# Two groups of output lines side by side in the PSUM banks: reordering the matmuls of an image convolution

## The reference

```
res = conv3x3(x, W_id, b_id)
cA, cH, cV, cD = _swt2_level3(x[0])
...
dmt = jnp.concatenate([low_att, high_att], axis=1)
out = jax.nn.leaky_relu(conv3x3(dmt, W_enc, b_enc), 0.01)
return out + res
...
x = x + _L0_conv_ref(_gn(x), ...)
```

## Time and profile before

| | |
|---|---|
| median of 3 runs | 1974.28 us (1973.63 to 1974.9) |
| the profiled execution | 1972.62 us |
| its span, first to last instruction | 1970.7 us |
| granted TensorE clock, mean | 0.998 |
| PE busy / PEld busy | 1941.7 us (99%) / 1548.0 us (79%) |
| DVE / ACT / POOL busy | 1470.2 / 997.5 / 1032.6 us |

### The profile page before, as it was taken

How to read it: one execution, slowest core, us unless ns; L and a number is a source line. 1 busy time by engine, 2 the same in 40 slices (tenths; PEclk the granted TensorE clock), 3 DMA queues, 4 the chain that set the end, 5 groups by cost and what they waited for, 6 DMA issues and landing times.

```text
span 1970.7 us, 79722 instructions
## 1 busy us (share of the span) xinstructions
PE 1941.7 (99%) x35638; PEld 1548.0 (79%) x35638; DVE 1470.2 (75%) x2253; ACT 997.5 (51%) x1062; POOL 1032.6 (52%) x774
## 2 busy tenths in 40 slices
PE   8999999999999999999999999999999999999998
PEld 7987999999999999766676667887666666776676
DVE  5665578778878776677777778777777777777776
ACT  4555666666666666644434444444444444344442
POOL 0005878887888786444444444444444444444444
PEclk9999999999999999999999999999999999999999
DMA  8883598888788884688887788887888888788774
GB/s 171 239 287 98 172 265 208 221 213 214 196 217 214 212 204 110 141 199 199 207 204 197 196 207 205 204 200 199 204 205 200 202 202 207 200 206 197 203 203 127
DMA packets 132635, 391.92 MB, mean 199 GB/s; under 512 B 49670, under 2 KB 50436, under 8 KB 118116
## 3 DMA queue, kind: packets, MB, share of 16 engines
q1 hardware_dynamic: 132324, 387.09, 77.4%
HBM read 258.56 MB, written 128.45 MB: 196 GB/s over the span
## 4 chain that ended last, share of the span: by engine, by line
PE 38%; issue 33%; POOL 26%; ACT 1%; POOLq 1%; DVE 1%; DMA 1%; SPq 0%; DVEq 0%; ACTq 0%
POOL stage L1660 25%; PE ps L1084 14%; PE ps L1054 7%; PE ps L616 5%; PE ps L1058 5%; PE ps L1057 3%; PE ps L618 3%; POOLq L1658 1%; PE ps L1067 1%; DMA big<-in_x 0%; DMA pool_of<-in_x 0%; POOL big L1354 0%; PE ps L582 0%; DVE pool_of L1255 0%; PE ps L508 0%
## 5 line engine op out<-in xcount | busy, mean ns | idle before, releaser
L1660 POOL TENSOR_TENSOR stage<-stage,big 128x448 f32<-128x448 f32 x448 | 511.8, 1143 | 640.9 <-DVE stage L1635 638.0
L1572 PE MATMUL ps<-pool_of,w_hi 64*64 64x448 f16 x12096 | 641.6, 350 | 4.8 <-issue 4.7
L1572 PEld LDWEIGHTS ps<-pool_of,w_hi 64*64 64x64 f16 x12096 | 413.5, 107 | 182.6 <-issue 9.1
L1572 PE MATMUL ps<-pool_of,w_lo 64*64 64x448 f16 x8064 | 449.2, 350 | 0.8 <-issue 0.7
L1572 PEld LDWEIGHTS ps<-pool_of,w_lo 64*64 64x64 f16 x8064 | 280.7, 107 | 118.5 <-issue 3.2
L1635 DVE SCALAR_TENSOR_TENSOR stage<-ps,w_max,pool_of 64x448 f32<-64x448 f32 x448 | 306.0, 683 | 44.0 <-PE ps L1572 31.3
L1635 DVE SCALAR_TENSOR_TENSOR stage<-ps,w_max,xs 64x448 f32<-64x448 f32 x384 | 262.3, 683 | 32.3 <-PE ps L1572 20.7
L1486 ACT ACTIVATE pool_of<-pool_of 128x2240 f16<-128x2240 f32 x56 | 126.5, 2260 | 313.3 <-PE ps L1572 313.3
L1255 DVE BATCH_NORM_STATS2 pool_of<-big 128x6 f32<-128x448 f32 x392 | 232.3, 616 | 70.7 <-DMA big<-in_x 70.5
L1486 ACT ACTIVATE pool_of<-xs,pool_of 128x2240 f16<-128x2240 f32 x48 | 108.4, 2258 | 283.5 <-PE ps L1572 283.5
L1572 PE MATMUL ps<-big,w_hi 64*64 64x448 f16 x4032 | 223.8, 350 | 0.0
(11 more groups left out here) (192 smaller groups left out, 2503.4 us busy)
## 6 DMA issues: line engine op xcount, KB each, us to landing
out<-stage SPq DMA_DIRECT2D x448, 224.0 KB, 3.2
big<-in_x SPq DMA_DIRECT2D x392, 224.0 KB, 5.1
pool_of<-in_x SPq DMA_DIRECT2D x104, 560.0 KB, 6.9
xs<-in_x SPq DMA_DIRECT2D x96, 560.0 KB, 7.4
pool_of<-row_filtered SPq DMA_DIRECT2D x110, 224.0 KB, 3.8
pool_of<-in_x SPq DMA_DIRECT2D x32, 392.0 KB, 7.9
row_filtered<-big SPq DMA_DIRECT2D x2, 6272.0 KB, 23.0
row_filtered<-big SPq DMA_DIRECT2D x4, 1568.0 KB, 9.5
```

The source lines that it names most:

```text
L1572: mm = pe.matmul(psum[4 * p + 2 * g + r][C * k:C * k + C, 0:NT], w[lanes, t, :], v[lanes, y:y + 2, kx:kx + W], start=(j == 0), stop=(j == ...
L1660: pool.tensor_tensor(stage[p][:, r, g, :], stage[p][:, r, g, :], e_map[:, e:e + NT], ALU.add)\
```

## The change

In `conv`, the loop over the groups g moves inside the loop over the 27 pieces. Before, the 108 matmuls of g = 0 ran over all pieces, and then the 108 of g = 1. Now each piece does its four matmuls for g = 0 (two banks) and then its four for g = 1 (the other two banks), so that four banks accumulate side by side. The signal `tiles` is still raised by the last matmul of each group, but these are now the fourth from last and the last of the band. Nothing else is changed; DVE's, ACT's, POOL's and SP's programs are the same, with line numbers one higher behind the edit.

```diff
-            for g in range(2):
-                for j, (w, v, t) in enumerate(pieces):
-                    ky, kx = t // 3, t % 3
+            for j, (w, v, t) in enumerate(pieces):
+                ky, kx = t // 3, t % 3
+                for g in range(2):
                     for r in range(2):
                         lanes = slice(C * r, C * r + C)
                         for k in range(2):
                             y = 4 * k + 2 * g + ky
                             mm = pe.matmul(psum[4 * p + 2 * g + r][C * k:C * k + C, 0:NT], w[lanes, t, :],
                                            v[lanes, y:y + 2, kx:kx + W], start=(j == 0), stop=(j == len(pieces) - 1))
-                mm.then_inc(tiles, 1)
+                    if j == len(pieces) - 1:
+                        mm.then_inc(tiles, 1)
```

## The result

The changed kernel takes 1981.21 us (median of 6 runs, 1979.46 to 1985.43), the kernel before 1973.95 us in 6 runs. The ratio is 1.0044 with a 95% interval of 1.0033 to 1.0055, so +6.5 to +10.9 us. The forecast was +0.14%, too little to be told from no change; the time is inside the range, but the kernel did become slower.

The account below looks back on a forecast made before the run. The prediction took TensorE to bound the kernel, at 98.4% of its column limit. Its terms, 0 + 0 + 2.86 = +2.9 us, gave 1975.5 us for the profiled execution and a median of 1977.1 us, range 1973 to 1982.5.

Parts of the forecast that it names:

- What TensorE does: Matmul pace in the image loop: same matmuls and weight loads, price 0, bounds 18.1 us gained or lost from bank changes.
- The signal of group 0, the split and the banks: In each band, DVE does eight read-outs in 5.69 us, then the split; TensorE still waits for neither split nor banks: 0.
- The read-out's followers: POOL's last addition and SP's stores and loads in each band move 2.86 us later, stores to R + 7.1; price 0.
- The loads' margin: Time between a load's landing and ACT's need in the tightest band: 3.7 us before, 0.85 us left after.
- DVE's lead: The split ends 1.7 us ahead of TensorE's need for it, 2.96 us before the change; cover shrinks, price 0.
- The end: After the last matmul, eight blocks are read instead of four, so all that follows is 2.86 us later.
- The pauses: PE's mid-band pauses, 9.9 us in all, read as late instructions during SP's transfers; expected change 0, bounds -9.9 to +9.9.
- rival B: In the loop, PE's pauses grow as the transfers run later; grown by half (+5), 1982 us; chance 20%.
- A: Rival: alternating banks or repeated weights remove TensorE's 3.0 ns a round over the column limit; 1959 us; chance 5%.
- C: Rival: DVE's lead before TensorE needs the split proves too small; 0.3 us a band gives 2010 us; chance 4%.
- D: Rival: pauses at bank changes halve TensorE's clock for one band in ten; about 2090 us; chance 1%.
- The sum: Whole kernel: 0 + 0 + 2.86 = +2.9 us, a median of 1977.1 us, +0.14%, no change that can be told.

Follow-up runs that it names:

- e2: Changed kernel, but both groups of a band accumulate into the same two banks; ratio 1.0036, 10.297 us a band.
- e3: Kernel before with group 0's signal at the band's end and banks alternating from piece to piece; ratio 0.9998, 10.246 us a band.
- f1: Kernel before with group 0's signal at the band's end, every second piece using the weights of the piece before it; 10.246 us a band.
- e4: Changed kernel, but group 1 reads the same input rows as group 0; ratio 1.0020, 10.247 us a band.
- e6: Kernel before with group 0's signal at the band's end, every second piece's data read two rows off; ratio 1.0021, 10.280 us a band.
- g3: Kernel before with late group 0 signal, all taps at column 0 and the same rows, but jumping two rows every round; 10.261 us a band.
- e8: Changed kernel with the groups in the order 0, 1, 1, 0 from piece to piece; ratio 1.0013, 10.269 us a band.
- e1: Kernel before, its matmul order kept, with only group 0's signal moved to the band's end; ratio 1.0016, 10.246 us a band.
- f3: Changed kernel, but the last of the 112 bands in the old order with group 0 signalled half-way; ratio 1.0015, 10.292 us a band.
- g2: Kernel before with group 0's signal at the band's end, every second piece's data read one row off; 10.268 us a band.
- e7: Changed kernel, but group 1 reads one row below group 0 instead of two; ratio 1.0015, 10.256 us a band.
- f4: Kernel before with the two x_hi products taken tap by tap and the last band stored in halves; ratio 0.9998, 10.248 us a band.
- e9: Kernel before with group 0's signal at the band's end, every tap reading the same rows from column 0; ratio 1.0004, 10.216 us a band.

## Why the prediction was wrong

- **What TensorE does: price 0. This is the step that failed.** It measured +6.0 us (112 x 0.054). I had kept +18.1 us as the upper bound, so the size was in sight, but I took 0 "since the group changes are the nearest rows". Those rows show 112 changes of group and the change makes some 54 in every band; a cost of 1 ns each can't be seen in one piece of 3.42 us. And I named the wrong candidates, bank and weights; where the data of each round starts stood nowhere in the working, so its price was put at nothing without a reason. e2 and e3 clear the banks, f1 and e4 the weights. What costs is that the moving data of each round starts two rows away from the round before (e4 takes it away and has the old pace, e6 and g3 put it in and lose 0.034 and 0.045 us, e8 takes half of it away and gets 57% back). In the old order the starts mostly move by one column or one row.
- **The signal of group 0, the split and the banks: right.** DVE's run of 5.69 us, the split right behind it, and PE waits for nobody. e1 shows that all the later work leaves the band at 10.246 us.
- **The read-out's followers: wrong in size, right in price.** The stores move from R + 4.2 to R + 9.4 and not to R + 7.1. I moved POOL's last addition beside the split and took its 1.14 us from a row beside nothing; it took 3.44. The loads' margin was gone with it, in 51 bands, and only DVE's lead of 1.7 us kept the price at 0. Had I named the neighbour, the margin would have been worked out as negative.
- **The end: right.** +2.86 us forecast, 12.3 - 9.5 = 2.8 us measured, and f3 takes it back.
- **The pauses: right as far as this comparison goes.** Loop less 112 clean bands leaves 10.0 us before and 9.9 us after. Over all profiled executions this rest was from 9 to 19 us (g2 9, e1 17, e7 19; f4, with the early signal, 16), so rival B was a real risk for one execution. An effect of the change on their sum isn't seen but can't be excluded below 3 us: e1 moves the transfers as the change does, and once the end's 2.8 us are taken off its total, +0.4 us are left (-1.8 to +2.7). Their place did move. Counting every round that lasts over 40 ns longer than usual, 17 of 18 pauses before lie 5.5 to 7.6 us behind the first matmul of a band (21 of 23 in f4), and 18 of 21 after lie 0.4 to 2.3 us behind it (22 of 24 in e1, up to 2.5 us). That is where 5.2 us of delay, which is what SP's stores got, would carry them over the band's end. So the pauses do come with SP's transfers, as the prediction supposed; that they are late instructions was only argued.
- **The rivals.** A was turned round: the remainder over the column limit grew. C and D did not come: PE never waited for DVE, and the granted clock stayed at 1.00 in the loop. The Trainium skill's figure, about 2.5 ns above N / 2.4 GHz per matmul (page "TensorE: Matmul & The Clock Gate", section "Wait — 56ns, not 53.3ns?"), is met by e9 alone, 10.216 us or 189.2 ns a round. The section calls this cost fixed for each matmul and doesn't speak of the weights. It isn't fixed here: the runs have 2.5 to 4.2 ns for a round of four.
- **The sum.** 6.0 + 2.8 = 8.8 us, in the measured +6.5 to +10.9. Several experiments (e3, e6, e8, f3) came out 2 to 4 us under their own sums, some just outside their intervals. With pauses that differ by up to 10 us from one execution to the next I rest the causes on the bands, not on the totals.

What stays open is the mechanism: why two rows cost more than one, why the bands have two levels, and why it's 0.054 us in the new order and 0.034 to 0.045 in the old. The new order also repeats each load of weights, and no run has its jumps without that.

## What to carry to other kernels

A loop order that uses each weight twice saves nothing where every matmul brings its own load and the loads are hidden; look at what else the order moves, and above all where the streamed operand starts from one matmul to the next. When a step is repeated thousands of times, a price of 0 needs a row that repeats it as often: one nanosecond a round was 6 us here. And when work is moved beside other work, take its duration from a row that has that neighbour.

## What the runs showed of the hardware

- The start column of the streamed float16 operand changes the pace of these matmuls. With all taps at column 0 a band takes 10.216 us, with all at column 1 10.306 us: 1.7 ns more for each round of four 64x448 matmuls. The real kernel has 18 of 27 taps at an even column and 9 at an odd one; two thirds of the one and a third of the other make 10.246 us, which is what it takes, and its own rounds show the difference (190.7 against 189.2 to 189.4 ns). By this about 3 us of the loop are due to those taps, and its pad of one column, which gives only the middle tap the odd start, would be the better parity; no run has another pad.
- A jump of two rows (904 bytes in a partition) at every round costs 0.03 to 0.054 us a band, a jump of one row (452 bytes) 0.010 to 0.022 us. In the new order the bands with the larger jump have two levels, near 10.28 and near 10.30 us.
- POOL's 128x448 addition takes 1.14 us beside DVE's read-outs from PSUM and 3.44 us beside the float32 subtraction of two SBUF operands.
- Alternating PSUM banks at every round, and repeating the weights at every second round in the old order, cost nothing (10.246 us each, e3 and f1).
- TensorE's pauses in the loop came with SP's transfers: when these ran 5.2 us later in the band, so did most of the pauses.
